# Hybrid layers: expert layers that prepare the next batch's rows beside the experts, and a linear attention whose PSUM banks are shared out as 2, 5 and 1

## The reference, cut to what matters

```python
# second and fourth layer: 8 experts, all computed for every row, the best 2 weighed in
probs = softmax(x @ Wr); topk_w, topk_idx = top_k(probs, 2); topk_w /= topk_w.sum(-1, keepdims=True)
for i in range(8):
    w_i = sum(topk_w * (topk_idx == i))
    h = silu(x @ Wg[i]) * (x @ Wu[i])        # 512x256 @ 256x256 twice, for each batch
    output += w_i * (h @ Wd[i])
# third layer: linear attention with decay, 16 query heads of 128 in 4 groups, one key and value head a group
q, k = rope(x @ wq.T), rope(x @ wk.T); v = x @ wv.T
for each chunk of rows:                       # one after another, with the state kv
    scores = (q_i @ k_i.T) * diag
    o = scores @ v_i + (q_i * q_dec) @ kv
    kv = blk * kv + (k_i * k_dec).T @ v_i
y = o @ wo.T
```

## Time and profile before

| | |
|---|---|
| median of 3 runs | 3113.7 us (3103.33 to 3115.58) |
| the profiled execution | 3112.98 us, of which the span is 3111.2 us |
| first expert layer | about 442 to 751 us: 309 us, PE busy 292.1 |
| linear attention | about 751 to 1291 us: 540 us, PE busy 498.9, DVE 301.8, ACT 55.6, POOL 240.7 |
| second expert layer | about 1291 to 1599 us: 308 us, PE busy 290.6 |

### The profile page before, as it was taken

The page is one execution under the profiler, slowest core; times in us unless marked ns, Lnnn a source line. Parts: engine busy times, 40 slices in busy tenths (PEclk is TensorE's granted clock), DMA queues, the critical chain, the costliest instruction groups (busy, mean ns, idle before and its releaser), DMA issues. The chain is left out here.

```text
span 3111.2 us, 45729 instructions
## 1 busy us (share of the span) xinstructions
PE 2809.1 (90%) x15592; PEld 1946.9 (63%) x15592; DVE 1653.8 (53%) x4517; ACT 843.2 (27%) x1368; POOL 991.8 (32%) x1105
## 2 busy tenths in 40 slices
PE   7999999999999999999978999999999658888876
PEld 3434458886555565688867888888887534443444
DVE  4566645666655656356654433343334566455556
ACT  2343344442111011244432222222222002222210
POOL 0000027775444434567750122222221011111211
PEclk8999999999999999999988999999999657887965
DMA  3000020000000000100000000000000000000000
GB/s 140 1 0 0 0 102 1 0 0 0 1 0 0 0 0 0 82 1 0 0 14 1 14 15 14 15 1 15 15 1 1 24 1 1 1 0 0 1 0 27
DMA packets 6288, 37.96 MB, mean 12 GB/s; under 512 B 272, under 2 KB 4368, under 8 KB 4496
## 3 DMA queue, kind: packets, MB, share of 16 engines
q1 hardware_dynamic: 6160, 36.34, 3.0%
HBM read 34.24 MB, written 2.10 MB: 12 GB/s over the span
## 5 line engine op out<-in xcount | busy, mean ns | idle before, releaser
L590 PE MATMUL banks<-back 32*128 32x512 f32 (+3 forms) x1088 | 367.9, 605 | 30.9 <-DVE back L600 21.3
L365 PE MATMUL banks<-moe_parts 128*128 128x512 f32 x1536 | 369.9, 397 | 13.8 <-POOL moe_parts L445 8.8
L817 ACT ACTIVATE back<-banks 128x1024 f32<-128x1024 f32 (+3 forms) x256 | 217.2, 863 | 464.0 <-PE banks L711 463.7
L365 PEld LDWEIGHTS banks<-moe_parts 128*128 128x128 f32 x1536 | 289.3, 192 | 77.2 <-issue 18.8
L1433 PE MATMUL banks<-lin_parts 128*128 128x512 f32 x1152 | 309.8, 415 | 19.3 <-DVE lin_parts L1689 15.5
L1624 DVE TENSOR_TENSOR ffn_pack<-banks,back 128x512 f32<-128x512 f32 x128 | 88.5, 692 | 391.8 <-PE banks L1446 391.7
L1433 PEld LDWEIGHTS banks<-lin_parts 128*128 128x128 f32 x1152 | 213.7, 194 | 77.9 <-issue 31.2
L711 PE MATMUL banks<-back 32*128 32x512 f32 (+3 forms) x1024 | 244.4, 591 | 19.6 <-DVE back L833 12.6
L590 PEld LDWEIGHTS banks<-back 32*128 32x128 f32 x1088 | 136.6, 201 | 188.0 <-DVE back L604 77.7
L1754 POOL TENSOR_TENSOR ffn_pack<-ffn_pack 128x256 f32<-128x256 f32 x112 | 82.5, 737 | 454.5 <-ACT ffn_pack L1587 453.0
L604 DVE TENSOR_REDUCE back<-banks 128x1 f32<-128x512 f32 x272 | 176.2, 687 | 80.7 <-PE banks L590 76.2
(11 more groups left out here) (235 smaller groups left out, 5166.9 us busy)
## 6 DMA issues: line engine op xcount, KB each, us to landing
back<-p_raw SPq DMA_DIRECT2D x8, 1024.0 KB, 4.8
back<-p SPq DMA_DIRECT2D x1, 7696.0 KB, 21.2
ffn_pack<-ffn SPq DMA_DIRECT2D x1, 6144.0 KB, 26.8
back<-p SPq DMA_DIRECT2D x1, 5152.0 KB, 15.1
back<-p SPq DMA_DIRECT2D x2, 1792.0 KB, 8.0
out<-x SPq DMA_DIRECT2D x1, 2048.0 KB, 7.5
x<-x_in SPq DMA_DIRECT2D x1, 1536.0 KB, 12.7
small_pack<-small SPq DMA_DIRECT2D x1, 619.0 KB, 4.9
```

Of the source, the lines that this page charges most:

```text
L365: mm = nc.tensor.matmul(bank[:], up[:, n % 2, a, which, kd, :], xp[:, b, kd, :], start=((a, b, kd) == (0, 0, 0)), stop=((a, b, kd) == (1, ...
L590: nc.tensor.matmul(bank[:, 0:n], qs[head_rows[j], hg, qi * P:(qi + 1) * P], ks[head_rows[j], hg, 0:n], start=True, stop=True).then_inc(D.f ...
L817: nc.scalar.activation(pt[:, (kt % 2) * 2 + pair, :, q0:T], two[:, :, q0:T], ACT.Exp, scale=0.25).then_inc(A.free.s, 2)
```

## The change

In the expert layers the two norm steps of a pair follow each other, so that the seven are done within the first four experts; `turn_xn` and `keep_xt` go ahead of the last but one `down`; and the rows of the next batch are split at the end of the loop, so that only the first batch's are split ahead of it. In the linear attention `A` gets two banks, `D` five and `O` one; `project` and `add_output` do one half at a call, the first half in step `n = 0`, the second in step `n = 1`.

```diff
 # moe_layer, TensorE
-                        if e + 1 == E2:
+                        if e + 2 == E2:
                             turn_xn(nc, c, pe, it)
                         down(e)
 # ScalarE
-                with act.Fori(0, B) as it:
-                    act.wait_ge(D.free.s, D.all_free(it))
+
+                def x_hi():
                     for kd in range(KD):
                         nc.scalar.activation(xp[:, 0, kd, :], c.xt[:, kd, :], ACT.Identity).then_inc(c.x_hi.s, 1)
+
+                act.wait_ge(D.free.s, D.all_free(0))
+                x_hi()
+                with act.Fori(0, B) as it:
                     act.wait_ge(c.lg_ready.s, c.lg_ready.at(it, 1))
...
                     hidden_hi(UNITS - 1)
+                    act.wait_ge(D.free.s, D.released(it, "xt", KD - 1))
+                    x_hi()
 # GpSimd: x_lo likewise, ahead of the loop and behind hidden_lo(UNITS - 1)
 # VectorE
                         if e + 1 < E2:
                             hidden(e + 1)
-                            norm[e]()
-                        else:
+                            for step in norm[2 * e:2 * e + 2]:
+                                step()
+                        if e + 2 == E2:
                             keep_xt(nc, c, dve, it)
                         weigh(e)
 # lin128_layer
-    D.take(c.banks[4:6])
-    O.take(c.banks[6:8])
+    A.take(c.banks[0:2])
+    D.take(c.banks[2:7])
+    O.take(c.banks[7:8])
...
                 for k, (g, n) in enumerate(steps):
                     for what in products_in(g, n):
                         product(*what)
-                    if n == 0 and g:
-                        project(g - 1)
+                    if n < 2 and g:
+                        project(g - 1, n)
                     if k + 1 < len(steps):
                         scores(*steps[k + 1])
                     grow_state(g, n)
                     output(g, n)
                 turn_xn(nc, c, pe, it)
-                project(G3 - 1)
+                for half in range(2):
+                    project(G3 - 1, half)
...
-                    if n == 0 and g:
-                        add_output(g - 1)
+                    if n < 2 and g:
+                        add_output(g - 1, n)
                 keep_xt(nc, c, dve, it)
-                add_output(G3 - 1)
+                for half in range(2):
+                    add_output(G3 - 1, half)
```

More of the change, by code:

```diff
@@ L441, in _, with x_lo @@
                         .then_inc(c.up_lo.s, 1)
-                with pool.Fori(0, B) as it:
+                def x_lo(it, first):
                     for kd in range(KD):
-                        pool.wait_ge(c.x_hi.s, c.x_hi.at(it, kd + 1))
+                        pool.wait_ge(c.x_hi.s, c.x_hi.at(it, first + kd + 1))
                         nc.gpsimd.tensor_tensor(xp[:, 1, kd], c.xt[:, kd], xp[:, 0, kd], ALU.subtract)\
                             .then_inc(c.x_lo.s, 1)
+                x_lo(0, 0)
+                with pool.Fori(0, B) as it:
                     def hidden_lo(n):
@@ L464, in _ @@
                     hidden_lo(UNITS - 1)
+                    x_lo(it, KD)
             @block.vector
@@ L541, in moe_layer @@
         c.up_lo.base += 2
+        c.x_hi.base += KD
+        c.x_lo.base += KD
 V_TILES = ((0, 1), (2,), (3,))
@@ L1107, in output, with project @@
                     mm.then_inc(A.full.s, 1)
[L1109 to L1119, removed]
+                def project(g, half):
+                    if half == 0:
+                        pe.wait_ge(A.free.s, A.released(it, "out", g, NT - 1))
+                    pe.wait_ge(O.free.s, O.may_fill(it))
+                    bank = O.fill("y", g, half)
+                    for i in range(2 * half, 2 * half + 2):
+                        for h in range(HQ):
+                            mm = nc.tensor.matmul(bank[:, (i % 2) * DM:(i % 2 + 1) * DM],
+                                                  ot[:, h, i * P:(i + 1) * P], wo[:, g * HQ + h, :],
+                                                  start=(h == 0), stop=(h == HQ - 1))
+                    mm.then_inc(O.full.s, 1)
                 for what in first_products:
@@ L1196, in keep_state, with add_output @@
                             .then_inc(D.free.s, 1)
[L1198 to L1206, removed]
+                def add_output(g, half):
+                    dve.wait_ge(O.full.s, O.may_read(it))
+                    bank = O.read("y", g, half)
+                    if g:
+                        dve.wait_ge(O.free.s, O.released(it, "y", g - 1, half))
+                    xs = c.x[:, it, 2 * half:2 * half + 2, :]
+                    nc.vector.tensor_tensor(xs, xs, bank[:].rearrange("p (a d) -> p a d", a=2), ALU.add)\
+                        .then_inc(O.free.s, 1)
                 for what in first_products:
@@ L1285, in lin128_layer @@
     now.close()
+    A.take(c.banks[0:4])
 def pack3(g):
```

## The result

The changed kernel takes 3069.7 us (median of 4 runs, 3066.46 to 3071.74) against 3109.05 (4 runs, 3103.33 to 3115.58): a ratio of 0.9875, with a 95% interval of 0.9851 to 0.9899. Its profiled execution took 3071.74 us, the span 3070.0; before it was 3112.98 and 3111.2. The forecast was 3074.0.

What follows compares the result with a forecast made beforehand. TensorE sets the linear attention's pace, idling for DVE; in the experts it waits for normed rows. -36.8 + 6.6 - 8.8 = -39.0 us from 3113.0 gives 3074.0, own range 3063 to 3086; 3060 to 3097 with smaller and larger gains.

Steps and rivals of the forecast that it cites:

- Five banks: Linear attention: scores and states no longer wait for DVE's rotation; 9.2 us a batch, 36.8 in four.
- the halves' price: Linear attention: the projection's second half waits for DVE's add on the single `O` bank; 6.6 us lost in four batches.
- The banks change nothing: Rival, linear attention: waits for the rotation only move to another DVE or GpSimd operation; 3110.8 us, chance 0.09.
- DVE becomes the bound: Rival, linear attention steps: DVE sets their pace, half of the 36.8 us is given back; 3092.4 us, chance 0.08.
- One bank for `O`: Linear attention projection: waits of 0.7 (last group) and 0.95 us (batch's end), none in groups 1 and 2; 6.6 us lost.
- Every second half waits: Rival, linear attention projection: 16 waits of 0.95 us, 15.2 us instead of 6.6; 3082.6 us, chance 0.12.
- slower: Rival, linear attention: single `O` bank puts TensorE behind all DVE has queued before the add; 3134.6 us, chance 0.06.
- Experts: Expert layers, turn of batches: the last `down` starts 1.1 us earlier, at eight turns; 8.8 us won.
- The row split's 0.36 us: Expert layers: wait ahead of the first unit goes, but the fourth unit waits 0.36 us longer for GpSimd; taken as 0.
- the experts win more: Rival, expert layers: the fourth unit's wait for GpSimd goes too; 3064.5 us, chance 0.07.
- The norm pairs: Expert layers: two norm steps at a time, DVE operations blocked beside GpSimd; taken as nothing, 11 us at most.
- The clock: Linear attention: two clock falls of 1.5 us go, two come at batch heads; net 0, 3 us either way.

Runs made afterwards that it cites:

- e5: Changed kernel with the linear attention's banks shared out as 3 for `A`, 3 for `D`, 2 for `O`: 3059.01 us in its one run.
- e1: Kernel before with only the expert layers' part of the change, linear attention as before: 3093.0 us, ratio 0.9955.
- e7: Changed kernel with banks 2, 4 and 2 (`A`, `D`, `O`) and three useless matmuls in each batch head's gap: 3065.01 us, ratio 0.9878.
- e4: Changed kernel with three useless matmuls in TensorE's gap at each batch's head: 3065.52 us, ratio 0.9883.
- e2: Kernel before with only the linear attention's part of the change, expert layers as before: 3068.95 us, ratio 0.9877.
- e3: Changed kernel with four banks for `D` and two for `O` in the linear attention: 3061.24 us, ratio 0.9869.

## Why the prediction was right, and where it was not

**Five banks: right.** Step (0, 1) now takes the 6.00 us of work, and the waits moved to no other operation. The prediction had three banks take up DVE's delay, without saying whether beside the old two or in all; e5 shows that three in all nearly do. With the halves' price, the two terms gave -30.2. Without the clock they are 507.7 less the 540.6 - 3.0 of before, -29.9, where 3.0 is the prediction's price of two falls; e1, the same code with one fall, took 538.9, so a fall cost 1.7 there and the sum may be -29.5. With two banks for `O` (e7, 500.5) it is -37.1, beside the 36.8 for `D` alone. *The banks change nothing* and *DVE becomes the bound* fall.

**One bank for `O`: right.** Two waits a batch, 0.52 and 0.78 us where 0.6 and 0.95 stood, none in the middle groups. With the refilling they cost 7.2 us in four batches where 6.6 was forecast. *Every second half waits* and *slower* fall: 8 of 16 halves wait. The page "Perfetto Trace Analysis" of the Trainium skill, section on matmuls, which wants groups to change banks, is borne out at those places and by the 7.2 us between e4 and e7.

**Experts: right.** In the windows they are -5.5 and -4.8, and seven of the eight turns give 1.0 to 1.1 us. Of the rest 1.5 is the first layer's last `down`, at the lower clock before and not now:

```profile
745.25 4.60 PE L379 MATMUL banks<-moe_parts 128*128 128x256 f32 x24
...
740.94 3.13 PE L379 MATMUL banks<-moe_parts 128*128 128x256 f32 x24 [0.59 <-POOL moe_parts L459]
```

What is left is 8.8, the forecast, but to the tenth by luck: the second layer's first turn is 1.7 us shorter here and 0.8 in e1, whose two layers give 5.4 and 3.8. The row split's 0.36 us are given back as forecast (0.51 and 1.22 us ahead of the third and fourth unit, the latter still 12.19 us after the router), so *the experts win more* falls too. The norm pairs cost nothing, as the timeline of DVE and GpSimd shows in the expert with six small operations:

```profile
478.79 1.28 POOL L459 TENSOR_TENSOR moe_parts<-moe,moe_parts 128x512 fp32r<-128x512 f32 x1
478.88 1.22 DVE L171 TENSOR_TENSOR rstd_sq<-rstd_sq,var_half 128x4 f32<-128x4 f32 x1
480.04 1.28 POOL L471 TENSOR_TENSOR moe_parts<-ffn_pack,moe_parts 128x512 fp32r<-128x512 f32 x1
480.13 1.21 DVE L172 SCALAR_TENSOR_TENSOR rstd<-rstd_sq,rstd 128x4 f32<-128x4 f32 x1
481.38 0.16 DVE L170 TENSOR_TENSOR rstd_sq<-rstd 128x4 f32<-128x4 f32 x1
...
482.16 1.66 DVE L530 SCALAR_TENSOR_TENSOR x<-banks,moe,x 128x256 f32 x4 [0.22 <-DVE rstd L172]
```

Those beside GpSimd last 1.2 us, one without it 0.16, and `weigh` (L530) ends at 483.82, when the next unit's product is there.

**The clock: the step that failed.** "I take two falls again, net 0" was mis-sized in the profiled execution, in number and in price: all four heads fall, at 2.3 us each on the mean where 1.5 was taken, so 9.2 us where 3.0 were lost before, +6.2. The idle 3.02 us itself was forecast (3.2). The Trainium skill, "TensorE: Matmul & The Clock Gate", section on oscillation, tells of a kernel whose clock fell at every one of its waits, of some 3 to 5 us. The changed kernel agrees, e2 does not: four equal gaps, one fall.

**The total came out so near by an offset, that is by luck.** The sum in the profile is -29.9 + 6.2 for the linear attention, -10.3 for the experts and -7.0 in the untouched stages: -41.0 of the measured -41.2, against -39.0. The prediction took the untouched stages for constant without saying so. They run at the lower clock for a part of their time (0.86 granted), and with the same matmuls PE was busy there for 1301 us (e5) to 1321 (e7). The lower end of the forecast's own range is 3064.4 by its terms, not 3063.

**Open.** Why the same 3.02 us drops the clock in one kernel and not in the other is not settled; all that differs is the expert layers, of which the one ahead ends 7 us earlier, and what follows from it. Nor is it settled whether the falls come in every execution. All four heads fall in both profiles of the changed kernel (516.9 and 516.8 us, the second with heads of 7.26, 7.43, 5.82 and 6.08) and in those of e3 and e5 (6.1 to 7.4), one of four in both of e2; yet the means over the runs show no clear gain from filling the gap.

## What to carry to other kernels

When two engines pass a ring of two banks to and fro in lock step, price the loss as the step's time less its work; a third bank took all but about 1 us of it here, and the fifth was better spent on the output. Taking a wait away brings only the time up to the next one: of the 2.02 us for the norm, 1.0 came. Judge each edit by the window of its own stage, and ahead of comparing totals look at the mean clock, since stages that nobody touched moved by 15 us; totals read at one clock leave out what an edit does to the clock itself.

## What the runs showed of the hardware

The same idle time of 3.02 us was followed by a granted clock of 0.59 and 0.75 at the first two heads of the changed kernel, and of 1.00 at the last three of the linear attention alone. The number of falls, four and one, came again in a second profile of each kernel. With three matmuls without use in the gap (2.74 us) the clock stayed at 1.00 in both profiles of e4. DVE operations on 128x4 numbers took 1.2 us beside a GpSimd operation of 1.28 and 0.16 without one.
